# Where the pieces for the row maxima stand in the long attention of a four-layer kernel

## The reference

```python
x = x + jnp.tanh(g_xattn[3]) * _L3_xattn_ref(_layernorm(x, axis=-1), ctx_512, ...)
...
q_r = jnp.einsum('bshq,hqr->bhsr', q_big, W_qr)
k_r = jnp.einsum('bld,hdr->bhlr', kv_rope, W_kr)
scores = jnp.einsum('bhsr,bhlr->bhsl', q_r, k_r)      # 16 heads, 56 rows, 1500 keys
attn = jax.nn.softmax(scores, axis=-1)
ctx_c = jnp.einsum('bhsl,bld->bhsd', attn, kv_rope)
```

## Time and profile before

| what | value |
|---|---|
| median of 3 runs | 2430.15 us (2428.51 to 2432.81) |
| the profiled execution's own time | 2433.71 us |
| its span, first to last instruction | 2431.9 us |
| busy in the span: TensorE matmuls | 2240.6 us, 92% |
| weight loads (PEld) | 1543.7 us, 63% |
| VectorE / ScalarE / GpSimd | 1566.2 us, 64% / 950.7 us, 39% / 805.0 us, 33% |
| granted TensorE clock, mean | 0.935 |

### The profile page before, as it was taken

How to read it: one execution, slowest core, us unless ns; L and a number is a source line. 1 busy time by engine, 2 the same in 40 slices (tenths; PEclk the granted TensorE clock), 3 DMA queues, 4 the chain that set the end, 5 groups by cost and what they waited for, 6 DMA issues and landing times. The chain is left out here.

```text
span 2431.9 us, 37375 instructions
## 1 busy us (share of the span) xinstructions
PE 2240.6 (92%) x13148; PEld 1543.7 (63%) x13148; DVE 1566.2 (64%) x2609; ACT 950.7 (39%) x1433; POOL 805.0 (33%) x471
## 2 busy tenths in 40 slices
PE   6768998989999998897999999898799999998998
PEld 4447997645555557664555555697455555567997
DVE  2765444378788856787888886412688888844444
ACT  2443443334444442212444444111344444424443
POOL 0321331024445440462444444001044544421332
PEclk9878999779999998897999999879799999998999
DMA  3473631464554513124545442286744544403332
GB/s 80 139 241 100 212 112 50 120 158 99 123 117 102 127 29 122 45 88 118 123 99 129 110 114 47 69 295 246 217 114 99 129 98 114 94 9 98 117 115 79
DMA packets 123790, 285.53 MB, mean 117 GB/s; under 512 B 33281, under 2 KB 76027, under 8 KB 119720
## 3 DMA queue, kind: packets, MB, share of 16 engines
q1 hardware_dynamic: 122984, 281.96, 43.6%
q0 software_dynamic: 672, 1.84, 0.2%
HBM read 237.15 MB, written 46.41 MB: 117 GB/s over the span
## 5 line engine op out<-in xcount | busy, mean ns | idle before, releaser
L1222 DVE TENSOR_REDUCE keep_top<-banks 128x1 f32<-128x500 f32 x945 | 615.5, 676 | 195.3 <-PE banks L1146 191.7
L1284 ACT ACTIVATE att_ex<-banks 125x896 f32<-125x896 f32 x576 | 515.6, 919 | 251.2 <-PE banks L1140 251.0
L1334 POOL TENSOR_TENSOR att_acc<-att_acc,att_two 125x896 f32<-125x896 f32 x186 | 393.2, 2114 | 420.4 <-DVE att_two L1237 407.1
L1171 PE MATMUL banks<-att_ex,att_v 125*64 125x448 f32 x2304 | 464.7, 545 | 0.0
L1146 PE MATMUL banks<-keep_kh,keep_qt 64*128 64x500 f32 x1008 | 381.7, 474 | 34.6 <-PEq L574 11.4
L1237 DVE TENSOR_TENSOR att_two<-att_ex 125x896 f32<-125x896 f32 x288 | 331.1, 1188 | 48.8 <-ACT att_ex L1284 48.6
L1171 PEld LDWEIGHTS banks<-att_ex,att_v 125*64 125x64 f32 x2304 | 152.5, 136 | 247.7 <-issue 212.3
L1140 PE MATMUL banks<-keep_qt,keep_kh 64*125 64x448 f32 x1152 | 303.4, 398 | 2.4 <-ACT att_ex L1284 2.4
L1146 PEld LDWEIGHTS banks<-keep_kh,keep_qt 64*128 64x128 f32 x1008 | 162.5, 195 | 216.6 <-DVE keep_top L1222 105.1
L1645 PE MATMUL banks<-moe_xs,moe_w 128*128 128x448 f32 x1272 | 283.1, 372 | 4.5 <-DVE moe_w L1741 2.9
L1140 PE MATMUL banks<-att_sh,att_on 64*125 64x448 f32 x1152 | 271.6, 366 | 0.0
(11 more groups left out here) (269 smaller groups left out, 2616.5 us busy)
## 6 DMA issues: line engine op xcount, KB each, us to landing
keep_kh<-kvt_hi SPq DMA_DIRECT2D x96, 375.0 KB, 5.1
att_kl<-kvt_lo SPq DMA_DIRECT2D x96, 375.0 KB, 7.2
q_rows<-mats_q SPq DMA_DIRECT2D x24, 896.0 KB, 5.1
keep_qt<-q_rows SPq DMA_DIRECT2D x96, 224.0 KB, 5.7
moe_raw<-L_experts_dram SPq DMA_DIRECT2D x53, 384.0 KB, 4.1
att_v<-kvn SPq DMA_DIRECT2D x24, 720.0 KB
sort_wu<-L_experts_dram SPq DMA_DIRECT2D x14, 1024.0 KB, 8.9
moe_cb<-comb_rows SPq DMA_DIRECT2D x62, 224.0 KB
```

Of the source, the lines that this page charges most:

```text
L1171: last = pe.matmul(PS[WEIGHED][64 * e:64 * e + 64, 0:HALF], v[:, s // 2, u, s % 2, :], ex[:, u % RING, e, :], start=u == 0, stop=u == UNIT ...
L1222: dve.tensor_reduce(top[:, s % 2, n // NS, n % NS:n % NS + 1], PS[6 + (PIECES * s + n) % 2][:, 0:SB], AX.X, ALU.max).then_inc(mx_done, 1)
L1284: act.activation(ex[:, u % RING], scored, ACT.Exp).then_inc(exp_done, 1)
L1334: pool.tensor_tensor(a, two[:, 0] if n == 1 else a, two[:, n % 3], ALU.add).then_inc(gathered, 1)
```

## The change

The same pieces, units and waits are issued in another order. `pieces` no longer takes a slot between units but one of 17 places, one ahead of each part of the group's four units and one behind the last. The function that issued a whole unit issues one part (two products); a unit's wait for its exponentials stands ahead of its part 0 and the count `st_ready` behind its part 3, as before. VectorE's loop takes the same places, so that its reductions keep their order. With | between parts the group becomes

```diff
@@ -1024,13 +1024,12 @@
             for s in range(4):
                 batch(s, B - 4 + s, min(2, 3 - s))
 
-        def pieces(i, slot, left):
-
-
+        PLACES = (0, 0, 6, 8, 10, 14, 16)
+
+        def pieces(i, place, left):
 
             ahead, base = ((1, NT), (1, 2 * NT), (2, 0))[i]
-            first = (0, 2, 3, 5, 6, 7)
-            return [(ahead, base + n) for n in range(first[slot], first[slot + 1]) if left >= ahead]
+            return [(ahead, base + n) for n in range(NT) if PLACES[n] == place and left >= ahead]
 
         def known(n, least):
             return isinstance(n, int) and n < least
@@ -1126,19 +1125,19 @@
                     return ((kh[rows, s, keys], high), (kl[rows, s % 2, keys], high),
                             (kh[rows, s, keys], ql[rows, s % 2, :]), (on[rows, :], sh[rows, s % 2, :]))
 
-                def scores(s, b, u, first):
-
-                    if not (known(b, 1) and u < 2):
+                def score(s, b, u, part, first):
+
+                    if part == 0 and not (known(b, 1) and u < 2):
                         pe.wait_ge(exp_done, UNITS * b + u - 1)
-                    for part in range(4):
-                        if u == 0 and part == 1:
-                            pe.wait_ge(kl_in[s % 2], of_two(s, b, 64))
-                        if u == 0 and part == 3:
-                            pe.wait_ge(m_in[s % 2], of_two(s, b, 64))
-                        for e in (first, 1 - first):
-                            k, rhs = products(s, u, e)[part]
-                            last = pe.matmul(PS[2 * (u % 2) + e][0:KP, 0:HALF], k, rhs, start=part == 0, stop=part == 3)
-                    last.then_inc(st_ready, 1)
+                    if u == 0 and part == 1:
+                        pe.wait_ge(kl_in[s % 2], of_two(s, b, 64))
+                    if u == 0 and part == 3:
+                        pe.wait_ge(m_in[s % 2], of_two(s, b, 64))
+                    for e in (first, 1 - first):
+                        k, rhs = products(s, u, e)[part]
+                        last = pe.matmul(PS[2 * (u % 2) + e][0:KP, 0:HALF], k, rhs, start=part == 0, stop=part == 3)
+                    if part == 3:
+                        last.then_inc(st_ready, 1)
 
                 def maxima(bank, s, n, half):
 
@@ -1183,12 +1182,12 @@
                 def batch(s, b, left):
                     for i in range(UNITS // 4):
                         half = 0
-                        for slot in range(5):
-                            if slot:
-                                scores(s, b, 4 * i + slot - 1, half)
-                            for ahead, n in pieces(i, slot, left):
+                        for place in range(17):
+                            for ahead, n in pieces(i, place, left):
                                 top_scores((s + ahead) % 4, b + ahead, n, half)
                                 half = 1 - half
+                            if place < 16:
+                                score(s, b, 4 * i + place // 4, place % 4, half)
                         for u in range(4 * i, 4 * i + 4):
                             weigh(s, b, u)
                         if i == 0 and not known(b, 1):
```

## The result

The changed kernel takes 2407.83 us (median of 4 runs, 2405.20 to 2408.97) against 2429.84 us for the kernel before: ratio 0.9905, 95% interval 0.9891 to 0.9919, 22 us less. The profiled execution took 2405.20 us, its span is 2403.4 us.

The account below looks back on a forecast made before the run. TensorE sets the pace, losing time where its matmul starts are held; 20.4 us saved less 1.0 and 1.5 given back is 18 us net, so 2412 us from the median 2430.15, range 2397 to 2425.

Parts of the forecast that it names:

- written out: Groups of batches outside the hardware loop: weighted sums at T+4.61 instead of T+4.81, 0.20 us saved in each of 60 groups.
- first looped groups: First group of each batch in the hardware loop: sums at T+4.77 against 4.94, 0.17 us saved in 24 groups.
- second and third looped groups: Later groups of batches in the hardware loop: sums at T+4.72, 0.09 us saved in each of 48 groups.
- The 15 us: TensorE's matmul row idles 0.34 us per batch; over 44 batches this reading allowed at most 15 us of gain.
- The hold that takes over: U2 waits for U0's exponential until T+2.32 in written-out groups, replacing the two removed waits of pieces on reductions.
- 2.29 us from the last hold, m4: Old group: m4 held until T+2.52 by m2's reduction, then a fixed 2.29 us to the weighted sums at T+4.81.
- The late third groups: Every other batch's third group, late because VectorE awaits a small DMA behind big loads: 1.5 us given back.
- The other term: Some 10 looped groups behind pair sums slowed by GpSimd's work: some 0.1 us late each, 1 us given back.
- A: Rival, larger gain: loop's register delays get hidden, every group reaches the sums at T+4.61; 33 us gain, 2397 us; chance 0.12.
- B: Rival, smaller gain: both row halves held at U3, sums 0.1 us later; gain 5 us, 2425 us; chance 0.10.
- D: Rival, no change: reductions still hold m3 in all groups, VectorE 0.4 us slower than read; 2430 us; chance 0.05.
- C: Rival, slower: a piece amid a unit breaks load-matmul overlap, 0.11 us each for m4 and m5; 2441 us; chance 0.09.

## Why the prediction was right, and where it was not

**The sum.** It forecast 2412 us from a gross gain of 20.4 us and 2.5 us given back, 18 us net; 22.0 us were measured. By groups, from the two timelines: written out 11.6 us in 57 groups (0.20 each, as forecast); first looped groups 4.5 us (0.19, forecast 0.17); second and third looped groups 0.13 each, forecast 0.09. That last term was mis-sized: U2 starts at T+2.40 where 2.43 was taken, and the rest of the group takes 2.27 us where 2.29 was taken; with 48 groups this is 2 us. These figures count the late groups in, and together they make the 20.5 us in the attention. The 15 us that the prediction reckoned from the matmul row's idle time were no bound. The span of the profiled execution fell by 28.5 us; the other 8 us lie outside these groups, where no instruction changed. Over the profiled executions of all ten kernels here span less attention lies between 1271 and 1282 us, with the kernel before at the upper end; so the 8 us are not put down to the change.

**The hold that takes over.** Right as told: the exponential of U0 stayed at T+1.35, U2 is held until 0.97 us after its start, and pieces wait on reductions only in third groups and in each layer's first group and the pieces ahead of it. The waits of piece loads fell to 26.5 us, forecast under 40.

**The chain before.** The prediction read the old group as "2.29 us from the last hold, m4". That gave the right number and half of the cause. With m2 put back alone, m4 is not held at all and the sums still stand at T+4.80. The old group was as long by two chains at once: m2's hold, U1, its exponential, U3; and m2's hold, its reduction, m4, U2. The group of the earlier trace rows (T = 533.80) shows the first of them in the exponential of U1 and the start of U3:

```profile
536.40 0.92 ACT L1284 ACTIVATE att_ex<-banks 125x896 f32<-125x896 f32 x1 [0.33 <-PE banks L1140]
```

```profile
537.46 0.43 PE L1140 MATMUL banks<-keep_qt,keep_kh 64*125 64x448 f32 x2
```

The exponential starts at T+2.60, so U3 could start at T+3.57 and the sums at T+4.80, as with m2 put back; behind m4's hold the queue reaches U3 at T+3.66 and the sums at T+4.81. The second chain hid the first. The prediction had U1's exponential in its steps for the new order, not for the old one, and so could not tell that either move alone gives nothing or costs 19 us. Since the change moves both pieces, the forecast held all the same, in that part by luck. The new order ends in two chains again: U2 at T+2.33 and 2.27 more, and U3 at T+3.35 and the 1.23 from there, T+4.60 and 4.58.

**What was given back.** The late third groups: 7.2 us beyond the usual before, 9.3 after, 2.1 more against 1.5 forecast (some tenths hang on what is taken as usual). The worst, in the changed kernel (T = 625.25), with VectorE's reciprocal as its releaser:

```profile
628.02 0.20 DVE L1242 RECIPROCAL att_rout<-att_rin 128x7 f32<-128x7 f32 x1 [3.05 <-DMA att_rin<-rs_rows]
```

```profile
628.89 0.49 PE L1145 MATMUL banks<-keep_kh,keep_qt 64*128 64x500 f32 x1 [1.93 <-DVE keep_top L1221]
```

The other term, 1 us for groups behind slow pair sums, did not appear: all first looped groups have m2 at T+1.54 to 1.56. The slack covers them.

**The rivals.** A: the loop's delay does not hide itself, looped groups stay at 4.67 and 4.76; it took the writing out to remove it. B: U3 is held for some 0.1 us on one half and restarts there (538.74 to 539.05), but the other half, which did m4, is as late without a hold, so no 0.1 us is lost. D: m3 is not held. C: 0.23 us lie between m4 and the next product on its half (538.23 to 538.46), the same as its own length at the pace of the earlier trace rows; a piece amid a unit costs no more than its own time.

## What to carry to other kernels

Before moving a step in a hand-written order, write down for one period the time at which each wait's condition is met and the time at which the queue arrives; the gain is set by the condition that is met next, here an exponential 0.2 us ahead of the old bound, and not by the waits that go. Do the same for the old order, since with two chains of like length a move that shortens only one of them pays nothing. The busy share of 92% did not show this; the starts did.

## What the runs showed of the hardware

- A matmul's load that has been held by a semaphore costs 0.10 us beyond the wait: the next product on the same half follows after 0.30 to 0.31 us instead of 0.20 to 0.21 (in the kernel with m4 put back 556.36 to 556.66, in the changed one 537.72 to 538.02).
- Inside the hardware loop an exponential starts up to 0.16 us later after the same matmul than in written-out code (T+1.51 against T+1.35), although no data differ; with the batches written out the delay is gone.
- A reduction of 128 x 500 lasts 0.68 us in the trace, but when reductions stand in a row the next one starts 0.59 to 0.67 us after it; a second reduction of the same piece cost 0.59 us of VectorE's queue.
- A transfer of 3.5 KB behind 2.9 MB of loads in the same queue made VectorE wait 26.6 us in all, in 18 of 45 cases; behind 2.2 MB it made it wait 0.2 us, once.
